# Lag attention: exponentials in PSUM, the down weight loaded one stage earlier and unpacked ahead of the loop, the ninth maximum used where it stands

## The reference

```
layer 2 ffn:       out = quantise_fp8(xn) @ quantise_fp8(weight), scaled back
layer 3 attention: corr = ifft(fft(q) * conj(fft(k))).real       per batch and channel, 128 lags
                   w, idx = top_k(corr, 9);  w = softmax(w)
                   out = sum_i w_i * v[min(idx_i + pos, 127)]    q = layernorm(x), k = v = context
layer 3 ffn:       a = x @ W1.T; b = x @ W3.T; out = (silu(a) * b) @ W2.T
```

## Time and profile before

| what | value |
|---|---|
| median of three runs | 1638.78 us |
| the profiled execution, its own time | 1639.02 us |
| span of the profiled execution | 1636.8 us |
| mean granted TensorE clock | 0.933 of full speed |
| busy over the whole span: PE, DVE, ACT, POOL | 1411.1, 1106.6, 732.0, 708.6 us |
| lag attention, from barrier to barrier | about 1303.5 to 1430 us of the span |

### The profile page before, as it was taken

One profiled execution on the slowest core, in us unless ns is written; L12 is line 12 of the kernel. 1 busy time (PEld: TensorE's weight loads), 2 busy tenths in 40 slices (PEclk: granted clock), 3 DMA queues, 4 the chain that ended last, 5 costly groups with the idle time before them and its releaser, 6 DMA issues. The chain is left out here.

```text
span 1636.8 us, 31565 instructions
## 1 busy us (share of the span) xinstructions
PE 1411.1 (86%) x11376; PEld 841.6 (51%) x11376; DVE 1106.6 (68%) x2221; ACT 732.0 (45%) x2378; POOL 708.6 (43%) x674
## 2 busy tenths in 40 slices
PE   5898499986999999769999999999986667559997
PEld 4775244435777776236555555556542243224443
DVE  7996565536666666658877877888776869665212
ACT  4775353213433332228665666666642245245110
POOL 4886541004333334306665666656650046643000
PEclk9998699997999999879999999999998679769998
DMA  7998481108999888337555456554432100275001
GB/s 191 179 173 150 99 163 39 22 6 177 173 177 164 150 136 144 85 118 149 111 113 136 107 109 137 117 107 98 82 78 101 36 18 18 41 156 94 10 1 51
DMA packets 516392, 172.51 MB, mean 105 GB/s; under 512 B 474784, under 2 KB 499680, under 8 KB 516112
## 3 DMA queue, kind: packets, MB, share of 16 engines
q1 hardware_dynamic: 516240, 170.51, 53.3%
HBM read 53.27 MB, written 2.10 MB: 34 GB/s over the span
## 5 line engine op out<-in xcount | busy, mean ns | idle before, releaser
L1627 POOL TENSOR_TENSOR a_q_ss<-a_q_ss,half 128x4 f32<-128x4 f32 x64 | 89.3, 1395 | 188.8 <-DVE a_q_ss L1557 95.1
L1487 ACT ACTIVATE a_probs<-a_masked,a_negmax 128x128 f32<-128x128 f32 x256 | 99.5, 390 | 94.6 <-DVE a_negmax L1532 94.6
L1072 POOL TENSOR_TENSOR a_p_hl<-a_probs,a_p_hl 128x512 f16<-128x512 f32 x64 | 74.1, 1158 | 155.2 <-DVE a_p_hl L1010 155.2
L67 PE MATMUL bank<-a_wq_hi,xn_hi 128*128 128x512 f16 (+1 forms) x384 | 139.6, 363 | 0.0
L68 PE MATMUL bank<-a_wq_lo,xn_hi 128*128 128x512 f16 (+1 forms) x384 | 139.5, 363 | 0.0
L69 PE MATMUL bank<-a_wq_hi,xn_lo 128*128 128x512 f16 (+1 forms) x384 | 139.4, 363 | 0.0
L67 PE MATMUL bank<-a_wo_hi,a_o_hi 128*128 128x512 f16 x256 | 97.0, 379 | 6.7 <-DVE x_state L1548 6.7
L69 PE MATMUL bank<-a_wo_hi,a_o_lo 128*128 128x512 f16 x256 | 97.0, 379 | 0.0
L68 PE MATMUL bank<-a_wo_lo,a_o_hi 128*128 128x512 f16 x256 | 97.0, 379 | 0.0
L1529 DVE TENSOR_TENSOR a_masked<-bank,a_mask 128x512 f32<-128x512 f32 x64 | 44.1, 689 | 72.9 <-PE bank L69 72.9
L1642 POOL TENSOR_TENSOR a_normal<-a_probs,a_recip 128x512 f32<-128x512 f32 x64 | 89.9, 1405 | 5.2 <-DMA a_p_t<-a_p_nat 0.3
(11 more groups left out here) (403 smaller groups left out, 5029.2 us busy)
## 6 DMA issues: line engine op xcount, KB each, us to landing
a_no<-in_L_xattn_Wo SPq DMA_DIRECT2D x9, 1024.0 KB, 5.7
a_nq<-in_L_xattn_Wq SPq DMA_DIRECT2D x8, 1024.0 KB, 6.0
f_n<-in_L_ffn_w SPq DMA_DIRECT2D x7, 512.0 KB, 4.3
f_n<-in_L_ffn_w2t SPq DMA_DIRECT2D x7, 512.0 KB, 4.7
a_n_wq<-in_L_xattn_Wq SPq DMA_DIRECT2D x4, 768.0 KB, 6.0
a_n_wo<-in_L_xattn_Wo SPq DMA_DIRECT2D x4, 768.0 KB, 5.9
a_nk<-in_L_xattn_Wk SPq DMA_DIRECT2D x9, 256.0 KB, 3.0
a_nv<-in_L_xattn_Wv SPq DMA_DIRECT2D x9, 256.0 KB, 3.0
```

The source lines that it names most:

```text
L67: pe.matmul(out, lh, rh, start=start, stop=False)
L1072: pool.tensor_tensor(p_hl[s % PN][:, 1, t, :], probs[unit(s, t) % PROBS][:, :, :].rearrange("p h n -> p (h n)"), p_hl[s % PN][:, 0, t, :], ...
L1487: m = act.activation(probs[s % 2][:, h, :], src, ACT.Exp, bias=negmax[s % 2][:, h:h + 1], accum_out=total[s % 2][:, h:h + 1])
L1627: pool.tensor_tensor(r[:, :], r[:, :], K.half[:, 0:n], ALU.pow).then_inc(root_done.sem, 1)
```

## The change

- The exponentials `e` go to PSUM bank 7, which this stage did not use, instead of SBUF. `picked` reads them there. ScalarE waits for `picked` of the batch before ahead of writing them.
- The negated maximum is computed on ScalarE instead of VectorE.
- `needle` is gone: the eight next maxima are kept in `next8`, and a fill overwrites places 1 to 7 behind the maxima; the second `match_replace` reads `next8` itself.
- The words and scales of the down weight are loaded at the end of the quantised layer's queue, into tensors that live through the three stages, and SP waits for them there.
- VectorE unpacks chunks 0 to 2 behind the statistics of batches 0 and 1, chunks 3 to 6 behind the normalisation of these two batches and the statistics of the other six (which stand there now), chunks 7 and 8 in step 0, and 9 and 10 in step 1. Steps 2 to 8 unpack nothing.
- ScalarE converts each chunk to f16 (`to_half`) right behind its unpacking, in place over its words. GpSimd scales from there into `flat` in the steps of `WHEN`, as before, and so do the steps of the halves and of the transposes.

```diff
@@ -2385,6 +2385,8 @@
             def _(sp):
                 spectra.load(sp)
                 sp.dma_start(nw[:, :, :], weight.rearrange("(k p) n -> p k n", p=P)).then_inc(inw, 16)
+                packed.load_down(sp, words_here)
+                sp.wait_ge(words_here, 32)
...
-        e, left8, left9 = sb("e", [P, KT, P]), sb("left8", [P, KT, P]), sb("left9", [P, KT, P])
-        top8, next8, needle = sb("top8", [P, KT, 8]), sb("next8", [P, KT, 8]), sb("needle", [P, KT, 8])
+        e, left8, left9 = K.bank[7], sb("left8", [P, KT, P]), sb("left9", [P, KT, P])
+        top8, next8 = sb("top8", [P, KT, 8]), sb("next8", [P, KT, 8])
...
+        UNPACK = {-2: (0, 1, 2), -1: (3, 4, 5, 6), 0: (7, 8), 1: (9, 10)}
...
-        own = Steps(K.sem("x3_own"), ["top8", "left8", "next8", "needle", "left9", "picked", "total"])
+        own = Steps(K.sem("x3_own"), ["top8", "left8", "next8", "alone", "left9", "picked", "total"])
...
-                down.load(sp)
                 for i in range(B + 3):
                     down.turn(sp, i)
                 down.wait_turned(sp)
...
-                    for chunk in down.at(i):
-                        down.to_float(act, chunk)
+                    for chunk in UNPACK.get(i, ()):
+                        down.to_half(act, chunk)
                     if l is not None:
                         act.wait_ge(t_bank.filled("x"), t_bank.n_filled("x", l))
                         act.activation(w_t[:, :], t_bank["x"][:, :], ACT.Copy).then_inc(t_bank.freed("x"), 1)
                     if m is not None:
+                        act.wait_ge(own.sem, own.count("top8", m))
+                        act.activation(negmax[:, :], top8[:, :, 0], ACT.Copy, scale=-1.0).then_inc(negmax_done.sem, 1)
                         act.wait_ge(negmax_done.sem, negmax_done.count("x", m))
+                        if m:
+                            act.wait_ge(own.sem, own.count("picked", m - 1))
                         for k in range(KT):
-                            i = act.activation(e[:, k, :], corr[1 - j][:, k, :], ACT.Exp, bias=negmax[:, k:k + 1])
+                            i = act.activation(e[:, k * P:(k + 1) * P], corr[1 - j][:, k, :], ACT.Exp, bias=negmax[:, k:k + 1])
                         i.then_inc(exp_done.sem, 1)
...
+                for i in (-2, -1):
+                    for chunk in UNPACK[i]:
+                        down.to_half(act, chunk)
                 over_steps(step)
...
-                    for chunk in down.at(i):
+                    for chunk in UNPACK.get(i, ()):
                         down.unpack(dve, chunk)
...
                         dve.wait_ge(own.sem, own.count("top8", m))
-                        dve.tensor_scalar(negmax[:, :], top8[:, :, 0], -1.0, None, ALU.mult).then_inc(negmax_done.sem, 1)
                         for k in range(KT):
                             i = dve.match_replace(left8[:, k, :], top8[:, k, :], values[:, k, :], GONE)
                         i.then_inc(own.sem, 1)
                         dve.wait_ge(own.sem, own.count("left8", m))
 
-                        dve.memset(needle[:, :, 1:8], GONE)
                         for k in range(KT):
                             i = dve.max(next8[:, k, :], left8[:, k, :])
                         i.then_inc(own.sem, 1)
                         dve.wait_ge(own.sem, own.count("next8", m))
-                        dve.tensor_copy(needle[:, :, 0:1], next8[:, :, 0:1]).then_inc(own.sem, 1)
-                        dve.wait_ge(own.sem, own.count("needle", m))
+                        dve.memset(next8[:, :, 1:8], GONE).then_inc(own.sem, 1)
+                        dve.wait_ge(own.sem, own.count("alone", m))
                         dve.memset(spacer[:, :], 0.0)
                         for k in range(KT):
-                            i = dve.match_replace(left9[:, k, :], needle[:, k, :], left8[:, k, :], GONE)
+                            i = dve.match_replace(left9[:, k, :], next8[:, k, :], left8[:, k, :], GONE)
                         i.then_inc(own.sem, 1)
                         dve.wait_ge(own.sem, own.count("left9", m))
                         dve.wait_ge(exp_done.sem, exp_done.count("x", m))
                         if m:
                             dve.wait_ge(weight_done.sem, weight_done.count("x", m - 1))
-                        dve.scalar_tensor_tensor(picked[:, :, :], left9[:, :, :], GONE, e[:, :, :],
+                        dve.scalar_tensor_tensor(picked[:, :, :], left9[:, :, :], GONE, e[:, :].rearrange("p (k n) -> p k n", k=KT),
...
                 take_stats(0)
-                take_stats(1)
+                for chunk in UNPACK[-2]:
+                    down.unpack(dve, chunk)
                 dve.wait_ge(eps_done.sem, eps_done.count("pow", 0))
                 for b in range(*AHEAD[0]):
                     dve.tensor_scalar(K.xn_rows[:, b, :], K.x[:, b, :], mv[:, b, 0:1], rstd[:, b:b + 1],
                                       ALU.subtract, ALU.mult).then_inc(first_done.sem, 1)
+                take_stats(1)
+                for chunk in UNPACK[-1]:
+                    down.unpack(dve, chunk)
                 over_steps(step)
...
+        self.words = stack.enter_context(K.nc.sbuf_tensor("down_words", [P, self.W2G * self.GROUP], I32))
+        self.scales = stack.enter_context(K.nc.sbuf_tensor("down_scales", [P, 2 * self.W2G], F32))
+
+    def load_down(self, sp, here):
+
+        w, s = self.source["w2"]
+        sp.dma_start(self.words[:, :], w.rearrange("(p g) c -> p (g c)", p=P)).then_inc(here, 16)
+        sp.dma_start(self.scales[:, :], s.rearrange("(p n) -> p n", p=P)).then_inc(here, 16)
...
-        self.words, self.scales = sb("words", [P, W.W2G * G], I32), sb("scales", [P, 2 * W.W2G], F32)
+        self.words, self.scales = W.words, W.scales
...
         g, G = self.groups(n), self.W.GROUP
         src = self.words[:, self.CHUNK // 2 * n:self.CHUNK // 2 * n + g * G].rearrange("p (j c) -> p j c", c=G)
         dst = self.ints[n % 2]
-        if n == 0:
-            dve.wait_ge(self.here, 32)
         if n >= 2:
-            dve.wait_ge(self.float_done.sem, self.float_done.count(n - 2))
+            dve.wait_ge(self.half_done.sem, self.half_done.count(n - 2))
         dve.tensor_scalar(dst[:, 0:g, 0, :], src, 4, None, ALU.arith_shift_right)
         dve.tensor_scalar(dst[:, 0:g, 1, :], src, 28, 28, ALU.logical_shift_left,
                           ALU.arith_shift_right).then_inc(self.ints_done.sem, 1)
 
-    def to_float(self, act, n):
+    def values(self, n):
+
+        at = self.CHUNK // 2 * n
+        return self.words[:, at:at + self.groups(n) * self.W.GROUP].bitcast(F16)
+
+    def to_half(self, act, n):
 
         act.wait_ge(self.ints_done.sem, self.ints_done.count(n))
+        act.activation(self.values(n), self.flat_row(self.ints, n), ACT.Copy, scale=WS).then_inc(self.half_done.sem, 1)
+
+    def scale(self, pool, n):
+
+        g = self.groups(n)
+        src = self.values(n).rearrange("p (j c) -> p j c", c=self.W.GROUP)
+        dst = self.flat[n % 2][:, 0:g, :, :].rearrange("p j h c -> p (j h) c")
+        by = self.scales[:, 2 * self.W.PER * n:2 * self.W.PER * n + 2 * g].unsqueeze(2).to_broadcast([P, 2 * g, self.W.GROUP])
+        pool.wait_ge(self.half_done.sem, self.half_done.count(n))
         if n >= 2:
-            act.wait_ge(self.lo_done.sem, self.lo_done.count(n - 2))
-        act.activation(self.flat_row(self.flat, n), self.flat_row(self.ints, n), ACT.Copy, scale=WS).then_inc(self.float_done.sem, 1)
-
-    def scale(self, pool, n):
-
-        g = self.groups(n)
-        rows = self.flat[n % 2][:, 0:g, :, :].rearrange("p j h c -> p (j h) c")
-        by = self.scales[:, 2 * self.W.PER * n:2 * self.W.PER * n + 2 * g].unsqueeze(2).to_broadcast([P, 2 * g, self.W.GROUP])
-        pool.wait_ge(self.float_done.sem, self.float_done.count(n))
-        pool.tensor_tensor(rows, rows, by, ALU.mult).then_inc(self.scaled_done.sem, 1)
+            pool.wait_ge(self.lo_done.sem, self.lo_done.count(n - 2))
+        pool.tensor_tensor(dst, src, by, ALU.mult).then_inc(self.scaled_done.sem, 1)
```

More of the change, by code:

```diff
@@ L2357, in _, with quantised_ffn @@
                     add_bias(b)
-def quantised_ffn(K, weight, spectra):
+def quantised_ffn(K, weight, spectra, packed):
     nc = K.nc
@@ L2377, in quantised_ffn @@
         inw, amax_done, whole_done, const_done = (K.sem(f"f2_{n}") for n in ("inw", "amax", "whole", "const"))
-        chain = K.sem("f2_chain")
+        chain, words_here = K.sem("f2_chain"), K.sem("f2_words")
         t_bank = Banks(K, "f2_t", K.bank[0:2], [0, 1])
@@ L2851, in __init__ @@
         step = lambda n: Steps(K.sem(f"down_{n}"), self.chunks)
-        self.ints_done, self.float_done, self.scaled_done, self.hi_done, self.lo_done = (
-            step(n) for n in ("ints", "float", "scaled", "hi", "lo"))
-        self.here, self.blank, self.turned = K.sem("down_here"), K.sem("down_blank"), K.sem("down_turned")
```

(27 more changed lines are left out.)

## The result

The changed kernel takes 1624.22 us (median of four runs, 1620.88 to 1625.19); the kernel before, run beside it on the same chip, 1638.36 (four runs, 1637.04 to 1641.01). The ratio is 0.9908, 95% interval 0.9889 to 0.9927: faster by 14.1 us, where 4.3 were forecast.

What follows compares the result with a forecast made beforehand. The prediction took VectorE to bound the loop over the batches. Start +7.5 and loop -11.75, all else at nothing, gave -4.3 us: 1638.78 became 1634.5, range 1629.5 to 1640.5.

Steps and rivals of the forecast that it cites:

- y(0) 7.5 late: Start of the lag attention: the unpacking moved there delays the first y matmul by 7.5 us.
- VectorE stands until GpSimd's first root: Start: VectorE idles until GpSimd's first root at 1315.07, as before, so three chunks (1.2 us) unpack there free.
- the edit that I took at nothing: Loading the down words behind the quantised layer's own load: 0 us, at the far end 8.6.
- My pairing: eight shifts in 5.1 us: Start, chunks 3 to 6: shifts meeting GpSimd operations wait for their end, so the eight run from 1320.2 to 1325.3.
- Four shifts in step 1, 4.1 us: Step 1, chunks 9 and 10: four shifts meet GpSimd's low halves and scalings, 1.0 to 1.1 us each.
- The loop: First to sixth y matmul: 48.0 us instead of 59.75, a gain of 11.75.
- The shorter ring of the prediction: Loop: y matmul 1.98, y copy and hand-over 0.7, GpSimd 6.42, given as 9.15 us a step.
- the first and the last interval: Loop's end intervals between y matmuls: first taken as 10.3 us, fifth as 9.8, against 9.3 for the others.
- stays: Tail behind the sixth y matmul: no VectorE work goes there, so its time is unchanged.
- (c): Rival, start: no collisions, shifts slip between GpSimd's small operations; net -11 us, 1628; chance 0.10.
- (a): Rival: the start, with PE at low clock, eats nearly all; net 0 to -3, 1637; chance 0.26 together with another rival.
- (b): Rival: PE at half clock for two more steps makes the kernel slower, +9.9 us, 1648; chance 0.12.

Runs made afterwards that it cites:

- the statistics run: The changed kernel with the statistics of batches 2 to 7 back in front of the wait for the first roots: 1623.73 us, ratio 0.9926.
- the kernel with both edits at the start: The changed kernel plus GpSimd's early small operation, with chunks 0-1 unpacked ahead of the normalisation, 2-7 in step 0, 8-10 in step 1: 1617.89 us.

## Why the prediction was wrong

**The step that failed** is the start, "y(0) 7.5 late". It was 0.5 early, 8.0 us off, and the prediction's own sign of it is there: the products of batch 0 come before 1323, at 1318.49. The terms, against the time from the first statistics on, 3.1 + 3.0 + 1.6 + 0.3:

- *VectorE stands until GpSimd's first root*, kept as it was. The root came 3.1 us earlier. What I read in the earlier trace rows as a wait for GpSimd's work was GpSimd's late start, which the small addition takes away, and with the words' transfer beside it it was longer: the run with the load alone moves the root from 10.13 to 7.39. That the transfer made it longer is what this run shows; how, it doesn't. It was also the edit that I took at nothing: I priced where the transfer went and not the place that it left.
- *My pairing: eight shifts in 5.1 us*. They took 2.1. Two errors: I let pow hold the third shift (1.4 us), and it held none of the four that met it; and the two scalings were to hold the sixth and seventh, but VectorE was through before they began, so that the next chunk's shifts met them (0.93 and 1.13) in a place where VectorE has time. The statistics of batches 2 to 7, 4.1 us, were on the path as forecast; moving them back gives 3.9 at the first products.
- *Four shifts in step 1, 4.1 us*. They took 2.5: two were held by low halves, 0.87 and 1.24, and the two of chunk 10, of 192 elements, were not.
- 0.3 us are left over, ahead of y(0).

**The loop** was right: 10.4, 9.06, 9.47, 9.05, 9.45 between the y matmuls, 47.43 us for 48.0, and two steps 18.53 and 18.50 for 18.63. (The shorter ring of the prediction adds up to 9.10 and not 9.15.) The ring was read rightly; the first and the last interval were estimates, one 0.1 too short and one 0.35 too long. `picked` at 0.69 throughout, exponentials in PSUM at 1.24 for four (1.28 in SBUF; a single one 0.35 for 0.39), the negated maximum at 0.21 on ScalarE, VectorE waiting 0.94 for the queries, GpSimd's scaling from f16 at 1.05, as from f32 before (1.04). How the 12.3 us divide is known in part: exponentials in PSUM 1.85, unpacking ahead 5.3, each against the changed kernel. The negated maximum and the needle were not run by themselves, and 5.2 are left for them only if the parts add up. The Trainium skill's rule that I weighed (GPSIMD Engine Reference, Key points) agrees in the loop, where `picked` with both inputs in SBUF took up to 1.49 us and with one 0.69. At the start the trace goes further: there GpSimd's addition was the one that waited (0.80 us), and pow held no shift.

**The tail**, "stays", was 2.75 shorter, by PE's clock: y(6) and y(7) at 1.98 and 1.95. That it is no property of the change is shown by the statistics run, which has the same tail and takes 21.16. So this part of the gain is luck as far as the prediction goes. y(6) goes with the product ahead of it. In the four traces with pr(7) at 3.78, PE idles for 1.7 us and y(6) takes 1.98; in the seven with pr(7) at 1.98 or 1.99 it idles for 3.1 to 3.9 and y(6) takes 2.60 to 3.78. (In the twelfth fillers stand right ahead of y(6), 1.88.) What sets pr(7) itself, and how much changes from one execution of a kernel to the next, is open, since each was traced once.

**Next stage and load.** 1.8 us came back behind the barrier, where PE waits for transposes by DMA; in every other kernel of this study it is 22.2 to 23.8 for 21.88 of before. Its cause wasn't tried. That the quantised weight lands 0.7 later (9.3 for 8.6) can't be told in the time: the stage began 0.7 earlier, and its start moves by 3.9 us between traces.

**Rivals.** (c) came nearest by its time, 1628, and its mechanism is half right: the shifts did slip between, but the scalings and halves hold as before. (a) is wrong: its condition, the queries of batch 1 and c(1) low, didn't occur (1.88 and 2.02 us). The first queries and c(0) ran low, but they did before too (3.78 and 3.65, and now 3.78 and 3.62), and the gap it feared as 7 us was 4.1. (b) didn't occur: 0.99 of the full clock in the loop.

## What to carry to other kernels

- An edit that takes a transfer or an operation away from a busy place has a price in two places. Work out what stood beside it there, above all a wait whose end the trace gives as "issue".
- Count a collision between two engines by who comes first and by the form of both instructions, not by the fact that they overlap. Where the outcome hangs on tenths of a microsecond in their order, the forecast is a range between none and all held, and that range belongs into the sum (1321.8 to 1329 by the prediction's own working, of which it took one pairing).
- This loop, bound by a ring, was forecast from rows to 1.2%. Its ends were not: the clock of a few short products moved the tail by 2.7 us between kernels that don't differ there, so a gain of that size needs both ends read before it is put down to an edit.

## What the runs showed of the hardware

- Behind the reduction over partitions GpSimd's next operation that wasn't a fill came late by 5.5 us in the changed kernel, by 6.7 to 7.6 in the three that do it at once, and by about 8.5 in the kernel before, with the words' transfer beside it. A fill started at once. A small addition put behind the reduction took this out of the later stage.
- A hold goes both ways: GpSimd's addition of 6 elements took 0.80 with VectorE's shifts beside it, 0.41 in the kernel before, 0.25 in the kernel with both edits at the start. Its pow of 6 elements, 1.35 us, held none of the four shifts that began inside it (0.29 each).
- A shift of 192 elements inside a GpSimd operation on 512 elements took 0.34, its usual time, while shifts of 256 and of 63 waited until the operation was over.
- Products of the same shape took 1.9 to 2.0 us at a granted clock of 1.00 and 3.6 to 3.8 at 0.50 (2.1 to 3.5 where it changed on the way). The long ones stood behind idle time of PE, but not each product behind idle time was long: c(0), 0.83 us behind the first queries, took 3.65 in the kernel before and 2.02 with the load alone moved. Filling a gap moved the long ones to another place more than it took them away.
